# The attention layer of a two-layer graph network on a clock of groups, with GpSimd adding the exponential blocks

## The reference, cut to what matters

```python
h = maximum(layernorm(x), 0)                   # before either layer
q, k, v = h @ Wq.T + bq, h @ Wk.T + bk, h @ Wv.T + bv      # 4 heads of 64
scores = clip(q . k / 8, -10, 10);  scores = where(adj == 0, -10, scores)
attn = softmax(scores in chunks of 256 keys)   # 8 chunks, each its own denominator
ctx = sum over the chunks of attn @ v
out = layernorm(ctx @ Wo.T + bo + h) * gamma + beta
x = x + out                                    # layer 0;  then layer 1 on x
```

## Time and profile before

| | us |
|---|---|
| median of 3 runs | 4936.84 |
| lowest run | 4935.59 |
| the profiled execution, its own time | 4939.3 |
| its span, first to last instruction | 4937.4 |

### The profile page before, as it was taken

One profiled execution on the slowest core, in us unless ns is written; L12 is line 12 of the kernel. 1 busy time (PEld: TensorE's weight loads), 2 busy tenths in 40 slices (PEclk: granted clock), 3 DMA queues, 4 the chain that ended last, 5 costly groups with the idle time before them and its releaser, 6 DMA issues. The chain is left out here.

```text
span 4937.4 us, 78171 instructions
## 1 busy us (share of the span) xinstructions
PE 4623.5 (94%) x31752; PEld 2710.8 (55%) x31752; DVE 3676.7 (74%) x5431; ACT 2913.0 (59%) x3370; POOL 1974.0 (40%) x1415
## 2 busy tenths in 40 slices
PE   7999999998998999999999899948999999999998
PEld 3334334333433433433333343328999999999998
DVE  4776676677578577667667757748889889898896
ACT  3553554555455355355455545518878888888785
POOL 3232233223232223223222323225657667666585
PEclk9999999999999999999999999969999999999999
DMA  5000000000000100000000000011212112111111
GB/s 188 9 9 9 26 18 9 26 9 18 26 9 9 35 9 9 9 26 18 9 26 9 18 9 9 9 42 43 65 41 70 46 53 76 34 65 60 41 57 44
DMA packets 126952, 160.50 MB, mean 33 GB/s; under 512 B 8832, under 2 KB 109184, under 8 KB 126592
## 3 DMA queue, kind: packets, MB, share of 16 engines
q1 hardware_dynamic: 126592, 155.49, 9.9%
HBM read 121.64 MB, written 33.83 MB: 31 GB/s over the span
## 5 line engine op out<-in xcount | busy, mean ns | idle before, releaser
L443 ACT ACTIVATE e_sb<-e_sb 128x1024 f32<-128x1024 f32 x1024 | 1080.4, 1056 | 1189.5 <-DVE e_sb L535 1174.2
L535 DVE SCALAR_TENSOR_TENSOR e_sb<-psS,mask 128x1024 f32<-128x1024 f32 x1024 | 1225.5, 1216 | 466.0 <-PE psS L650 459.2
L1251 PE MATMUL psA<-xy,ring_p 128*128 128x195 bf16 x8192 | 1404.3, 249 | 13.2 <-DVE red L1131 13.2
L1251 PE MATMUL psA<-xy,ring_s 128*128 128x195 bf16 x8192 | 1403.7, 249 | 0.0
L650 PE MATMUL psS<-qT,kT 64*128 64x512 f32 x4096 | 1087.7, 616 | 41.6 <-DVE e_sb L535 41.6
L1051 ACT ACTIVATE ring_s<-eiB,ejb 128x1024 int8<-128x1024 f32 x1024 | 1088.5, 1135 | 9.6 <-PE psA L1251 9.6
L663 PE MATMUL psN<-e_sb,v_sb 128*64 128x512 f32 x4096 | 1002.4, 611 | 0.0
L374 POOL TENSOR_TENSOR ctxT<-ctxT,num 128x512 f32<-128x512 f32 x384 | 486.5, 1276 | 1009.0 <-DVE num L513 1009.0
L1251 PEld LDWEIGHTS psA<-xy,ring_p 128*128 128x128 fp8e4 x8192 | 801.9, 98 | 19.2 <-DVE red L1131 16.4
L1251 PEld LDWEIGHTS psA<-xy,ring_s 128*128 128x128 fp8e4 x8192 | 800.6, 98 | 8.6 <-issue 0.3
L650 PEld LDWEIGHTS psS<-qT,kT 64*128 64x128 f32 x4096 | 460.0, 187 | 448.0 <-issue 233.2
(11 more groups left out here) (106 smaller groups left out, 4020.4 us busy)
## 6 DMA issues: line engine op xcount, KB each, us to landing
eiB<-ei_between SPq DMA_DIRECT2D x64, 512.0 KB, 4.2
xin<-x SPq DMA_DIRECT2D x32, 512.0 KB, 6.8
xr<-x SPq DMA_DIRECT2D x32, 512.0 KB, 3.8
x_between<-hy SPq DMA_DIRECT2D x32, 512.0 KB, 2.9
xin<-x_between SPq DMA_DIRECT2D x32, 512.0 KB, 5.6
xo<-x_between SPq DMA_DIRECT2D x32, 512.0 KB, 4.4
out<-o_sb SPq DMA_DIRECT2D x32, 512.0 KB, 5.3
xr<-adjT SPq DMA_DIRECT2D x12, 512.0 KB, 4.8
```

The lines of the kernel that those rows point to most:

```text
L443: act.activation(e_sb[:, s % ES], e_sb[:, s % ES], ACT.Exp, scale=SCALE).then_inc(exp_done, 1)
L535: dve.scalar_tensor_tensor(out=e_sb[:, s % ES], in0=psS[:, s % 2], scalar=-CLIP_RAW, in1=mask[:, kb, cols][:, None, :].to_broadcast([P, 2, ...
L1251: ins = pe.matmul(psA[:, i % BANKS, br * PARTS * XW:(br + 1) * PARTS * XW], part[:, n % RING, k, tt * TW + j * P:tt * TW + (j + 1) * P], x ...
```

## The change

- The clock of the four programs is now a group k (two steps), 64 in a batch and 9 in the gap (GAPG). `half_at` and `tile_at` say which half or tile is at an offset after its end; `alive` runs the end of the last batch beside the start of the next one.
- The denominators are taken from e_sum. GpSimd adds the two key blocks' exponentials of each group (`sum_blocks`, 128 x 1024 float32) into one of three buffers; TensorE then needs four matmuls for a chunk where it had eight. They are issued in odd k, behind the numerators.
- The numerators' two matmuls of 64 columns in a step become four of 32.
- VectorE issues the two clips of a group ahead of most else of it. The eight broadcasts and multiplies of a half lie at the offsets in PICKS: at = 0 is ahead of scores and clips, at = 1 behind them. The quarters of the reciprocal lie at offsets 2, 2, 3, 3, the split at 4; the tile's norm at 12 to 17, its scaling at 20 and 21, GpSimd's last work at 28 and 29.
- The next batch's input norms are spread: statistics at k = 6 to 9 and 22 to 25, one Newton chain for all 16 blocks (not four) at k = 54 to 57.
- xr and hy are doubled; SP loads residuals two tiles ahead. Beta is added to xr (in k of HB_AT + 1), so the end of a tile has two GpSimd operations where it had three.
- e_sb has 8 slots (6 before), num 13 (11 before). A clip waits for the numerators and for e_sum of the group four before. The input of the batch after next is loaded earlier.
- In the first batch 14 strips are converted ahead of the groups and 10 beside them (LATE).

```diff
-LAG = 2
-ES = 6
-NS = GPH + 3
+GROUPS = BSTEPS // KPC
+ES = 8
+SUMS = 3
+NS = 13
...
+GAP, GAPG = 18, 9
+READ_AT, INV_AT, SPLIT_AT = 2, (2, 2, 3, 3), 4
+PICKS = ((5, 1), (6, 0), (6, 1), (7, 1), (8, 0), (8, 1), (9, 1), (10, 1))
+RES_AT, HB_AT = 1, 4
+OUT_AT, STAT2_AT, AGGR2_AT, RSQRT2_AT = 11, 12, 14, (15, 15, 16, 17)
+YN_AT, AFFINE_AT = 20, 28
+TAILG = GROUPS + AFFINE_AT + 2
+XSTATS_AT, RSQRT_AT, TURN_AT = (6, 8, 22, 24), (54, 55, 56, 57), (58, 59, 60, 61)
...
+        e_sum = sb("e_sum", [P, SUMS, 2, TW])
-        xr = sb("xr", [P, TB, F])
-        hy = sb("hy", [P, TB, F])
+        xr = sb("xr", [P, 2, TB, F])
+        hy = sb("hy", [P, 2, TB, F])
...
+        def half_at(k, off):
+            h, r = divmod(k - off, GPH)
+            return h - 1 if r == 0 and 1 <= h <= HALVES else None
+        def tile_at(k, off):
+            t, r = divmod(k - off, 2 * GPH)
+            return t - 1 if r == 0 and 1 <= t <= T else None
+        def picked(k, where):
+            return [(half_at(k, off), i) for i, (off, at) in enumerate(PICKS)
+                    if at == where and half_at(k, off) is not None]
+        def alive(b, k):
+            return [(b, k)] + ([(b - 1, k + GROUPS + GAPG)] if b and k + GROUPS + GAPG < TAILG else [])
...
         @block.gpsimd
+            def sum_blocks(b, g):
+                n = b * GROUPS + g
+                pool.wait_ge(exp_done, KPC * (n + 1))
+                if n >= SUMS:
+                    pool.wait_ge(sums_done, (n - SUMS) // PAIRS + 1)
+                pool.tensor_tensor(e_sum[:, n % SUMS], e_sb[:, KPC * n % ES], e_sb[:, (KPC * n + 1) % ES], ALU.add)\
+                    .then_inc(esum_done, 1)
...
+                for k in groups_of(b):
+                    if 1 <= k <= GROUPS:
+                        sum_blocks(b, k - 1)
+                        if b == 0 and k <= LATE:
+                            convert_strip((T - 1) * STRIPS - LATE + k - 1)
+                    for bb, kk in alive(b, k):
+                        for where in range(2):
+                            for half, i in picked(kk - 1, where):
+                                add_to_ctx(bb, half * GPH + i)
+                        affine(bb, kk)
...
         @block.vector
+                for k in groups_of(b):
+                    for bb, kk in alive(b, k):
+                        take_output(bb, kk)
+                        for half, i in picked(kk, 0):
+                            normalize(bb, half * GPH + i)
+                    if k < GROUPS:
+                        clip(b, 2 * k)
+                        clip(b, 2 * k + 1)
+                    for bb, kk in alive(b, k):
+                        for half, i in picked(kk, 1):
+                            normalize(bb, half * GPH + i)
+                        invert(bb, kk)
+                        norm_output(bb, kk)
+                    if b + 1 < nb:
+                        next_norms(b + 1, k)
...
         @block.tensor
-                for i in range(2):
-                    hd = 2 * pair + i
-                    ins = pe.matmul(psN[64 * i:64 * i + 64, pair, :], v_sb[:, kb, hd * D:(hd + 1) * D],
-                                    e_sb[:, u % ES, i, :], start=u % KPC == 0, stop=u % KPC == KPC - 1,
+                    for part in range(4):
+                        i, col = part // 2, (2 * pair) * D + 32 * part
+                        ins = pe.matmul(psN[32 * part:32 * part + 32, pair, :], v_sb[:, kb, col:col + 32],
+                                        e_sb[:, n % ES, i, :], start=u % KPC == 0, stop=u % KPC == KPC - 1,
...
-                for hd in range(H):
-                    slot = (u - KPC * (PAIRS - 1 - hd // 2)) % ES
-                    ins = pe.matmul(psD[32 * hd:32 * hd + 32, :], hot[:, c, :],
-                                    e_sb[:, slot, hd % 2, :], start=first, stop=last,
+                pe.wait_ge(esum_done, PAIRS * (n + 1))
+                for hd in range(H):
+                    ins = pe.matmul(psD[32 * hd:32 * hd + 32, :], hot[:, c, :],
+                                    e_sum[:, (PAIRS * n + hd // 2) % SUMS, hd % 2, :], start=c == 0, stop=c == CPH - 1,
...
+                    for bb, kk in alive(b, k):
+                        for half, i in picked(kk, 0):
+                            broadcast(bb, half, i)
+                    if k < GROUPS:
+                        scores(b, 2 * k)
+                        scores(b, 2 * k + 1)
+                    for bb, kk in alive(b, k):
+                        for half, i in picked(kk, 1):
+                            broadcast(bb, half, i)
+                    if 1 <= k <= GROUPS:
+                        numerators(b, k - 1)
+                    if k % 2 and 3 <= k < GROUPS + 2:
+                        denominators(b, (k - 3) // 2)
+                    for bb, kk in alive(b, k):
+                        project(bb, kk)
```

More of the change, by code:

```diff
@@ L188, in layer0 @@
         oproj_done = sem("oproj_done")
-        xr_in = sem("xr_in")
+        xr_in = [sem(f"xr_in{i}") for i in range(2)]
         hr_done = sem("hr_done")
@@ new lines, in invert @@
+            def invert(b, k):
+                for j in range(TB):
+                    half = half_at(k, INV_AT[j])
+                    if half is not None:
+                        h = b * HALVES + half
+                        cols = slice(j * P, (j + 1) * P)
+                        if j == 0:
+                            dve.wait_ge(sums_read, h + 1)
+                        ins = dve.reciprocal(r_f[:, cols], r_f[:, cols])
+                        if j == TB - 1:
+                            ins.then_inc(inv_done, 1)
+                half = half_at(k, SPLIT_AT)
+                if half is not None:
+                    h = b * HALVES + half
+                    dve.wait_ge(inv_hi_done, h + 1)
@@ L669, in denominators, with numerators @@
-            def denominators(b, u):
-                if not 0 <= u < BSTEPS or place(u)[1] != PAIRS - 1:
-                    return
-                c = u // SPC % CPH
-                first, last = u % HALF == KPC, u % HALF == HALF - 1
-                if first and u >= HALF:
-                    pe.wait_ge(sums_read, b * HALVES + u // HALF)
+            def numerators(b, g):
+                for u in (2 * g, 2 * g + 1):
+                    (kb, pair), n = place(u), b * BSTEPS + u
+                    pe.wait_ge(exp_done, n + 1)
+                    if u % KPC == 0 and g >= PAIRS:
+                        pe.wait_ge(numcopy_done, b * GROUPS + g - 1)
+                    for part in range(4):
+                        i, col = part // 2, (2 * pair) * D + 32 * part
+                        ins = pe.matmul(psN[32 * part:32 * part + 32, pair, :], v_sb[:, kb, col:col + 32],
+                                        e_sb[:, n % ES, i, :], start=u % KPC == 0, stop=u % KPC == KPC - 1,
+                                        skip_group_check=True)
+                ins.then_inc(num_done, 1)
@@ L712, in step, with broadcast @@
-            def step(b, s):
-                if s > BSTEPS:
-                    project(b, s)
-                    broadcast(b, s)
-                    return
-                if s % 2:
-                    return
-                if s == BSTEPS and b + 1 < nb:
-                    turn(b + 1, 0, False)
-                project(b, s)
-                broadcast(b, s)
-                scores(b, s)
-                scores(b, s + 1)
-                if s < BSTEPS:
-                    broadcast(b, s + 1)
-                for of in (numerators, denominators):
-                    of(b, s - LAG)
-                    of(b, s + 1 - LAG)
+            def broadcast(b, half, i):
+                h = b * HALVES + half
+                if i == 0:
+                    pe.wait_ge(r_done, h + 1)
+                if i == 0 and h >= 2 and h % 2 == 0:
+                    pe.wait_ge(y_done, h)
+                elif h or i:
+                    pe.wait_ge(norm_done, h * GPH + i)
+                rows = slice(64 * (i % PAIRS), 64 * (i % PAIRS) + 64)
+                pe.matmul(psM[:, :], pick[rows, i, :], r_s[rows, :], start=True, stop=True).then_inc(bcast_done, 1)
@@ new lines, in project @@
+            def project(b, k):
+                for j in range(2):
+                    t = tile_at(k, OUT_AT + j)
+                    if t is not None:
+                        n = b * T + t
+                        if j == 0:
+                            pe.wait_ge(ctx_done, b * CTX + ctx_until(2 * GPH * (t + 1) - 1))
+                        else:
+                            pe.wait_ge(y_done, 2 * n + 1)
+                        for a in range(2):
+                            col = (2 * j + a) * P
+                            for pair in range(PAIRS):
+                                ins = pe.matmul(psM[:, a * F:(a + 1) * F], ctxT[:, pair, col:col + P],
+                                                w_o[:, pair, :], start=pair == 0, stop=pair == PAIRS - 1)
+                        ins.then_inc(oproj_done, 1)
```

469 lines of the change are left out of this document (233 added, 236 removed).

## The result

| | before | after | ratio (95% interval) |
|---|---|---|---|
| median, us | 4937.84 | 4861.02 | 0.9845 (0.9825 to 0.9864) |
| span of the profiled execution | 4937.4 | 4859.4 | |

The changed kernel is 1.55% faster: 77 us, where 286 were forecast, and above the stated range of 4530 to 4800. The gain is clear of the noise, but it is under the 2% from which the prediction speaks of faster. One of the four executions of before took 12565 us and is left out of the ratio; without it the median of before is 4936.84, with it 4937.84. A batch of layer 0 takes 392.9 us after 402.1, not 366.7.

The account below looks back on a forecast made before the run. It took TensorE's own work as the bound, waiting for VectorE. A batch of 402.1 us less 29.8, 19.05 and 3.6 gave 349.7, plus 17 of stalls 366.7; 283 us saved over eight, so 4651 us, range 4530 to 4800.

Parts of the forecast that it names:

- The denominators: On TensorE, a chunk's eight matmuls become four: 0.93 us saved a chunk, 29.8 us a batch, 238 us over eight.
- the numerators: On TensorE, four instructions of 64 columns become eight of 32: still 1.86 us, so 0 us of change.
- the sum on GpSimd: Sixty-four sums of 128 x 1024 a batch at 2.370 us each, 151.7 us, with GpSimd's load staying under PE's.
- The stalls that I keep: Step for PE's remaining stalls in a batch: 4 us a tile, 16 a batch, and 1 for backlog, 17 us.
- the split and scalings: VectorE work at offsets 20 and 21 beside GpSimd's back-to-back operations: PE loses about 2.5 us in each tile.
- ScalarE's slot: ScalarE waiting for a free slot of num, once a tile for two groups, holding back two exponentials: 1.5 us a tile.
- the backlog: On GpSimd in groups 19 and 20, where old and new tile's work meet: 2.4 us of backlog, put at 1 us a batch.
- the floor: A layer 0 batch of 349.7 us: 402.1 less 29.8 for denominators, 19.05 of PE idle time and 3.6 of low clock.
- the first count: 41 VectorE instructions a batch exposed to waiting out GpSimd operations, 43 us as upper estimate; the forecast went by it.
- the second count: 80 exposed VectorE instructions a batch, adding every instruction of a Newton chain and the split; used for the lock-heavy rival.
- lock-heavy: Rival: 80 exposed instructions at 1.05 us lengthen VectorE by 84 us a batch, about half showing; 4814 us, chance 0.2.
- The slower rivals: VectorE becomes the bound, 5440 us, chance 0.05; narrow numerators do not run four abreast, 5650 us, chance 0.03.

Follow-up runs that it names:

- e1: Changed kernel without GpSimd's sums, denominators taken from e_sb by eight matmuls a chunk, rest of the new order kept: 4761.6 us, ratio to before 0.9638.
- e2b: e1 plus GpSimd additions of the same size at the same place, from constant buffers, that nobody waits for: 4944.1 us.
- e3: Changed kernel with sums over one of the two heads alone, 128 x 512, the first head's denominators used twice: 4618.9 us.
- e5: Changed kernel with GpSimd's additions to ctxT issued ahead of the same group's sum, not behind it: 4854.2 us.
- e6: Changed kernel with the four scalings of a tile's norm on ScalarE, one tiny product more on VectorE: 4764.1 us, ratio to before 0.9651.
- e12: Changed kernel with the three Newton steps of both norms left out, reciprocal roots left at their first guess: 4746.1 us.
- e9: Changed kernel with ctxT additions ahead of sums, scalings on ScalarE, and groups 14, 15 and 0 of a tile's 16 not summed: 4680.9 us.
- e4: Changed kernel with the numerators back at two matmuls of 64 columns in a step: 4862.1 us.
- e11: e9 with group 1 also taken directly and the next batch's Newton chain moved from groups 54-57 to 46-49: 4618.8 us, ratio to before 0.9352.

## Why the prediction was wrong

- **The denominators, the numerators, the sum on GpSimd: right.** 0.97 for 0.93, 1.74 to 1.85 for 1.86, 2.390 for 2.370. The wait for e_sum by PE, taken as nothing, is 1.8 us a batch.
- **What failed is the step "The stalls that I keep".** It had 17 us a batch: 2.5 a tile for the split and scalings, 1.5 for ScalarE's slot, 1 for the backlog. Idle time and low clock make 46.9. That GpSimd's sums make the stalls was right (e1, e2b, e3). What PE pays for them was mis-sized, and most of it in terms that the step did not have:

| PE, us a batch | forecast | measured |
|---|---|---|
| behind split and scalings | 10 | 11.5 |
| ScalarE late (slot of num) | 6 | 4.5 |
| ctxT late (backlog) | 1 | 5.3 |
| hT late (ScalarE) | 0 | 3.4 |
| clips | 0 | 3.1 |
| other multiplies, e_sum, v_sb | 0 | 5.4 |
| low clock | 0 | 13.7 |

- *The clock.* This is the largest term. I took 3.6 us of low clock out of the floor and put none back for the new stalls, though my own rows had the clock at 0.50 behind a wait of 2.0 us. It falls four times in a batch, not once, behind waits of 2.98, 4.40, 4.39 and 3.37 us.
- *The scalings.* The sum over a batch came out near the forecast by luck. It had four tiles at 2.5 us. The trace has two tiles at 1.36 + 4.40 us, and two with next to nothing. I read the four in 2.33 us as one wait for four instructions. GpSimd beside them did one operation of 1.37 us, with a pause behind it:

```profile
1611.97 1.37 POOL L367 TENSOR_TENSOR ctxT<-num 128x512 f32<-128x512 f32 x1 [2.52 <-DVE num L513]
1614.82 1.28 POOL L374 TENSOR_TENSOR ctxT<-ctxT,num 128x512 f32<-128x512 f32 x1 [1.47 <-DVE num L513]
```

  In the changed trace each of two scalings waits for an operation of its own: GpSimd gets its turn between them. The forecast had waits of 2 and 1 us; they are 1.9 at the split and 4.1 at the two scalings. A row taken beside one operation with a pause behind it does not show what happens beside a queue without pauses.
- *The queue.* ctxT was taken as 1 us a batch of backlog. It is 5.3 us in the list, and hT's 3.4 goes with it (both are gone in e5). e5 shows that undoing it alone brings only 7 us in all.
- *Which instructions are exposed, and for how long.* The forecast went by the first count, 41. L93 and L95 (L86 and L88 before) at 0.600 and 0.410 us, which are 0.160 and 0.162 without the sums (e1), show that the second count, 80, was the right one. The rule of the Trainium skill (SBUF — State Buffer, "Who interferes with whom"), that an instruction with two SBUF inputs contends with a GpSimd instruction that reads SBUF, agrees with these rows. I had given it 0.2. But the price was far under either count's: the sums lengthen VectorE's work by 16 us a batch, not by 43 or 84 (286.4 us of the 302.3 are there without them, where the forecast had 275). A mean rest of an operation for each exposed instruction is too much; the medians stay near quiet (L639 0.744, L664 0.407), and a few instructions wait for 2 us.
- The rival "lock-heavy" was right in kind, and of the rivals with a sum its 4814 us is the nearest. It had half of 84 us of VectorE's growth shown, 37 over the floor. In truth 16 us of growth, in the wrong places and with the clock behind them, put 43 us over the floor. VectorE did not become as full as PE. The slower rivals did not happen.
- *The new order's own gain* I had folded into the floor. It is real: 176 us by itself (e1). That e1 meets the floor within 1.1 us a batch is in part luck: 5.6 us of waits stay in it, and PE's work is less than I had by about as much, 3.5 us of it from the numerators in front of denominators. The chance of faster by over 2%, 0.83, rested on a loss of 17 where 43 came.

Not settled: how the 337 us of the sums divide by place. Scalings 97, chain 115 and queue 7 are each from one undoing; they need not add, and some 120 us have no run of their own. e6 and e12 also take the instructions themselves off VectorE, so they do not test the waits alone; e3, e9 and e2b, which leave VectorE's work as it is, do. Why real sums cost 155 us more than dummy ones, and why e4's clock is higher, is open.

## What to carry to other kernels

Work given to an engine with time to spare is paid for where it meets the others, not by its own load. Here the sums, with GpSimd busy for 65% of the span, lengthened VectorE's work by only 16 us a batch and still cost TensorE 337 us in all. Keeping a quarter of them away from the few exposed instructions, and moving some of those to ScalarE, won back 242 of these (e11). Look for each exposed instruction with the length of what will run beside it then, not of what ran before. Here the four longest stalls of a batch, 3.0 to 4.4 us each, were paid again at half clock behind them, so a budget of stalls needs both terms.

## What the runs showed of the hardware that was not expected

- The clock had a third of the price: 13.7 us at 0.50 beside 33.2 us of idle time in a batch of 392.9, behind four waits of 2.98 to 4.40 us. In e1 and e11 no such stretch is in the batch, and more than half of what e6 gained is clock.
- Back-to-back VectorE instructions do not keep GpSimd out: between two scalings with no wait between them GpSimd started a 2.40 us operation (1419.76), and the second waited it out.
- Matmuls of 32 columns divide among four column places, and the fullest place sets the time: 12 instructions in 1.82 us, 16 in 1.83, 8 in 0.97.
- Numerators of 32 columns in front of denominators of 32 columns take 1.74 us, 1.85 in front of scores; numerators of 64 columns take 1.87 in front of either. The Trainium skill (TensorEngine Tiling (Array Packing), "Key Properties") says that a change of tiling mode drains the array; the 0.11 us agrees with it.
